# The causal limit of two attentions: from TensorE masks and a VectorE minimum to a position select on GpSimd

## What is computed

```python
xn = layernorm(x)                      # x: 8 batches x 256 tokens x 256
# branch 1 ("MLA"): 16 heads, 64 rotary + 16 plain dimensions
q, k = concat(q_c, rope(q_r)), concat(k_c, rope(k_r))
attn = softmax(q @ k.T * 80**-0.5 + causal mask)
s = (attn @ v) @ w_out.T
# branch 2: rmsnorm, 16 heads of 16 dimensions ("MHA"), then top 2 of 8 experts
attn = softmax(where(causal, q2 @ k2.T * 16**-0.5, -inf))
x2 = xn + (attn @ v2) @ Wo.T
g = silu(x2 + moe(rmsnorm(x2)))
out = x + s * g
```

## Time and profile before

| | us |
|---|---|
| median of 3 runs | 969.01 (966.42 to 970.13) |
| the profiled execution | 961.99 |
| its span, first to last instruction | 960.2 |
| busy in the span: PE, DVE, ACT, POOL | 836.7, 655.9, 502.4, 285.3 |
| one loop iteration (a batch) | 77.3 |

### The profile page before, as it was taken

The page is one execution under the profiler, slowest core; times in us unless marked ns, Lnnn a source line. Parts: engine busy times, 40 slices in busy tenths (PEclk is TensorE's granted clock), DMA queues, the critical chain, the costliest instruction groups (busy, mean ns, idle before and its releaser), DMA issues.

```text
span 960.2 us, 20067 instructions
## 1 busy us (share of the span) xinstructions
PE 836.7 (87%) x6688; PEld 747.9 (78%) x6688; DVE 655.9 (68%) x2335; ACT 502.4 (52%) x1091; POOL 285.3 (30%) x282
## 2 busy tenths in 40 slices
PE   5879999999999998999999999977179999999980
PEld 3868988887887797797898788865169999998980
DVE  4877667667767857866866766763237777777754
ACT  2435365365356356446536535634047777676751
POOL 5520310330221131041032023001314565645641
PEclk9988999999999999999999999988579999999995
DMA  9000000000000000000000000030146677779836
GB/s 277 1 1 1 13 1 25 14 1 13 12 11 2 23 11 2 22 12 1 23 12 1 13 16 7 13 141 15 36 151 184 183 238 202 224 232 334 248 49 186
DMA packets 40159, 70.88 MB, mean 74 GB/s; under 512 B 10946, under 2 KB 35138, under 8 KB 37122
## 3 DMA queue, kind: packets, MB, share of 16 engines
q1 hardware_dynamic: 29074, 57.39, 17.7%
q0 software_dynamic: 9856, 12.13, 6.5%
q10 hardware_dynamic: 1152, 0.49, 0.3%
HBM read 55.25 MB, written 14.81 MB: 73 GB/s over the span
## 4 chain that ended last, share of the span: by engine, by line
PE 51%; DVE 14%; DMA 14%; issue 14%; POOL 3%; ACT 2%; SPq 1%; DVEq 0%; POOLq 0%; ACTq 0%
PE ps L575 40%; DMA expert_rows<-yo,slot_of 11%; PE ps L668 6%; PE ps L705 3%; DVE ps L1400 2%; DVE ps L1403 2%; POOL expert_rows L552 1%; DVE negm L1403 1%; PE ps L601 1%; DMA ln<-in_w_ln 1%; DVE negm L1400 1%; POOL xg L541 1%; PE ps L610 1%; DMA xg<-x_normalised,slot_of 1%; PE ps L805 1%
## 5 line engine op out<-in xcount | busy, mean ns | idle before, releaser
L1094 ACT ACTIVATE ex<-ps 128x384 f32<-128x384 f32 x256 | 125.2, 494 | 130.4 <-PE ps L575 128.9
L575 PE MATMUL ps<-qt,kt 128*128 128x256 f32 (+1 forms) x768 | 163.8, 324 | 4.5 <-issue 3.2
L505 POOL TENSOR_TENSOR tok<-tok,swp 128x256 f32<-128x256 f32 x128 | 97.2, 760 | 219.3 <-DVE swp L1355 218.3
L1400 DVE CUSTOM_DVE_ANT_0 ps<-ps,mask 128x128 f32<-128x128 f32 x256 | 76.2, 298 | 70.4 <-PE ps L575 42.6
L1403 DVE CUSTOM_DVE_ANT_0 ps<-ps,mask 128x256 f32<-128x256 f32 x256 | 118.5, 463 | 0.7
L575 PEld LDWEIGHTS ps<-qt,kt 128*128 128x128 f32 x768 | 109.3, 193 | 11.9 <-issue 7.0
L1234 DVE TENSOR_TENSOR wel<-raw,weh 128x768 fp32r<-128x768 f32 x92 | 88.1, 958 | 34.4 <-ACT weh L962 34.4
L552 POOL DMA_INDIRECT expert_rows<-yo,slot_of x46 | 77.9, 1693 | 104.7 <-DMA expert_rows<-yo,slot_of 54.8
L575 PE MATMUL ps<-wh,xth 128*128 128x320 f32 (+2 forms) x352 | 95.5, 353 | 5.9 <-DVE wl L1234 3.3
L1351 DVE TENSOR_TENSOR tok<-ps,cos_t 128x320 f32<-128x320 f32 x128 | 62.7, 490 | 52.3 <-PE ps L575 46.4
L962 ACT ACTIVATE qt<-ps 128x512 f32<-128x512 f32 (+1 forms) x96 | 57.0, 594 | 61.3 <-PE ps L668 54.6
(11 more groups left out here) (164 smaller groups left out, 1965.8 us busy)
## 6 DMA issues: line engine op xcount, KB each, us to landing
raw<-in_w_experts SPq DMA_DIRECT2D x23, 1536.0 KB, 7.2
mla_branch<-s_b SPq DMA_DIRECT2D x8, 256.0 KB, 2.1
expert_rows<-xn SPq DMA_DIRECT2D x8, 256.0 KB, 2.2
x_normalised<-otk SPq DMA_DIRECT2D x8, 256.0 KB, 2.1
xr<-in_x SPq DMA_DIRECT2D x1, 2048.0 KB, 14.8
s_tok<-mla_branch SPq DMA_DIRECT2D x1, 2048.0 KB, 14.2
w_cols_raw<-in_w_cols SPq DMA_DIRECT2D x1, 1792.0 KB, 15.6
x<-expert_rows SPq DMA_DIRECT2D x3, 512.0 KB, 5.1
```

Source lines behind the costliest of these rows:

```text
L505: nc.gpsimd.tensor_tensor(t, t, swp[:, n % 2, :, :], ALU.add).then_inc(tokd, 1)
L575: return nc.tensor.matmul(o, a, m, start=start, stop=stop, skip_group_check=True, **k)
L1094: nc.scalar.activation(ex[:, h % (2 * G), :], ps[4 + h % 2][:, P:4 * P], ACT.Exp, scale=scale).then_inc(ex_, 1)
L1400: nc.vector.tensor_tensor_reduce(out=o[:, 0:P], in0=o[:, 0:P], in1=mask2[:, 1, :], scale=-1.0, scalar=-2.0 * BIG, op0=ALU.add, op1=ALU.min ...
```

## The change

All 256 diagonal columns of each head's exponentials are limited on POOL, in T1 and in T2, by `affine_select`: it keeps an element where query minus key is not negative and writes 0 elsewhere. T2's `values` therefore wait for a new semaphore `exm2`. DVE's minimum, T2's two mask matmuls a head, two constant loads and two casts go. POOL's order becomes, for each batch: 16 selects of T1 with `power2` after head 6, the 16 rotary sums, 16 selects of T2 with one slot scatter after each of the heads 9, 10, 11 and 12.

```diff
+            def causal(b, ex_, exm, after):
+                for h in range(H):
+                    wait(pool, ex_, 16 * b + h + 1)
+                    pool.nop(nofuse=True)
+                    a = ex[:, h % (2 * G), 0:2 * P].rearrange("p (a q) -> p a q", a=2)
+                    nc.gpsimd.affine_select(a, a, [[0, 2], [1, P]], ALU.is_ge, zero, 0, -1).then_inc(exm, 1)
+                    after.get(h, lambda: None)()
+            def slots_between(r):
+                return {9 + 2 * t + k: lambda t=t, k=k: scatter_slot(r, t, k) for t in range(2) for k in range(2)}
+            zero = nc.gpsimd.to_reg(0.0)
+            causal(0, ex1, exm1, {})
             rope_sums(1)
+            causal(0, ex2, exm2, {})
             pool.wait_ge(s_slot, 16)
             with pool.Fori(1, last) as b:
-                power2(b - 1)
+                causal(b, ex1, exm1, {6: lambda: power2(b - 1)})
                 rope_sums(b + 1)
-                scatter_slots(b - 1)
-            power2(last - 1)
-            scatter_slots(last - 1)
+                causal(b, ex2, exm2, slots_between(b - 1))
+            causal(last, ex1, exm1, {6: lambda: power2(last - 1)})
+            causal(last, ex2, exm2, slots_between(last - 1))
             power2(last)
-            scatter_slots(last)
+            for t in range(2):
+                for k in range(2):
+                    scatter_slot(last, t, k)
...
             def scores2(h, o):
-                mm(o[:, 0:2 * P], kt2[:, h // 2, P:S], qt2[:, h, :], True, False)
-                mm(o[:, 2 * P:4 * P], kt2[:, h // 2, 0:P], qt2[:, h, :], False, False)
-                mm(o[:, P:2 * P], idb[:, :], maskb[:, :], False, True)
-                return mm(o[:, 2 * P:3 * P], idb[:, :], maskb[:, :], False, True)
+                mm(o[:, 0:2 * P], kt2[:, h // 2, P:S], qt2[:, h, :], True, True)
+                return mm(o[:, 2 * P:4 * P], kt2[:, h // 2, 0:P], qt2[:, h, :], True, True)
...
-                heads(b, scores2, st2, ex2, ex2, pv2, ov2, v2, before_h0, lambda: wait(pe, sd, b + 1), max_head,
+                heads(b, scores2, st2, ex2, exm2, pv2, ov2, v2, before_h0, lambda: wait(pe, sd, b + 1), max_head,
...
-            for dst, src in ((idf[:, :], ident), (mask_f[:, 0, :], mask), (mask_f[:, 1, :], mask_t),
-                             (seen[:, 0, :], seen_t), (cos_t[:, :, :], cosines), (sin_t[:, :, :], sines),
+            for dst, src in ((idf[:, :], ident), (mask_f[:, :], mask),
+                             (cos_t[:, :, :], cosines), (sin_t[:, :, :], sines),
...
-            def causal(b, h):
-                wait(dve, ex1, 16 * b + h + 1)
-                a = ex[:, h % (2 * G), 0:2 * P].rearrange("p (a q) -> p a q", a=2)
-                nc.vector.tensor_tensor(a, a, seen[:, 0:1, :].broadcast_to([P, 2, P]), ALU.min).then_inc(exm1, 1)
             def stage_m2(b, after):
                 wait(dve, mtr2, b)
                 for h in range(H):
-                    causal(b, h)
                     maxima(b, h, (h % 2) * (H // 2) + h // 2, negm2, m2d, mx2)
```

More of the change, by code:

```diff
@@ L56 @@
 BIG = -1e30
-BOUND = 1e30
 IT = FF // P
@@ L92, in build @@
 def build(nc, x, w_cols, w_dq, w_uqr, w_dkv, w_ukv, w_out, w_o, w_ln1, w_ln2, w_r, w_experts,
-          cosines, sines, ident, mask, mask_t, seen_t, upper, route_c, slots, out):
+          cosines, sines, ident, mask, upper, route_c, slots, out):
     ctx = ExitStack()
@@ L161, in build @@
         prep = ExitStack()
-        mask_f = sb("mask_f", [P, 2, P], F32, prep)
+        mask_f = sb("mask_f", [P, P], F32, prep)
         up_f = sb("up_f", [P, P], F32, prep)
@@ L171, in build @@
         kt = sb("kt", [P, H, S], F32, early)
-        seen = sb("seen", [P, 1, P], F32, late)
-        idb = sb("idb", [P, P], BF16, late)
-        maskb = sb("maskb", [P, P], BF16, late)
         mask2 = sb("mask2", [P, 2, P], BF16, late)
@@ L263, in build @@
         exm1 = sem("mla_exp_masked")
+        exm2 = sem("mha_exp_masked")
         pv1 = sem("mla_pv")
@@ L513, in power2, with scatter_slot @@
                 nc.gpsimd.tensor_tensor(rstd2[:, :], msq2[:, :], mhalf[:, 0:2], ALU.pow).then_inc(rm2, 1)
-            def scatter_slots(r):
-                pool.wait_ge(posd, r + 1)
-                pool.nop(nofuse=True)
-                for t in range(2):
-                    for k in range(2):
-                        nc.gpsimd.indirect_dma_start(slot[:, :], bass.IndirectOffsetOnAxis(posu[:, t, k:k + 1], 0),
-                                                     meta[:, t, k, :], None).then_inc(msc, 16)
+            def scatter_slot(r, t, k):
+                if t == 0 and k == 0:
+                    pool.wait_ge(posd, r + 1)
+                    pool.nop(nofuse=True)
+                nc.gpsimd.indirect_dma_start(slot[:, :], bass.IndirectOffsetOnAxis(posu[:, t, k:k + 1], 0),
+                                             meta[:, t, k, :], None).then_inc(msc, 16)
+            def causal(b, ex_, exm, after):
+                for h in range(H):
+                    wait(pool, ex_, 16 * b + h + 1)
+                    pool.nop(nofuse=True)
+                    a = ex[:, h % (2 * G), 0:2 * P].rearrange("p (a q) -> p a q", a=2)
[5 more added lines that the diff above has]
+            causal(0, ex1, exm1, {})
             rope_sums(1)
+            causal(0, ex2, exm2, {})
             pool.wait_ge(s_slot, 16)
             with pool.Fori(1, last) as b:
-                power2(b - 1)
+                causal(b, ex1, exm1, {6: lambda: power2(b - 1)})
                 rope_sums(b + 1)
-                scatter_slots(b - 1)
-            power2(last - 1)
-            scatter_slots(last - 1)
+                causal(b, ex2, exm2, slots_between(b - 1))
+            causal(last, ex1, exm1, {6: lambda: power2(last - 1)})
+            causal(last, ex2, exm2, slots_between(last - 1))
             power2(last)
-            scatter_slots(last)
+            for t in range(2):
+                for k in range(2):
+                    scatter_slot(last, t, k)
             def gather(blk):
@@ L864, in _ @@
                 if m == 1:
-                    pe.wait_ge(s_k, 16 * 8)
+                    pe.wait_ge(s_k, 16 * 6)
                     transpose_x(0)
@@ L884, in _ @@
             pe.wait_ge(s_c, 16 * 4)
-            pe.wait_ge(cast, 3)
+            pe.wait_ge(cast, 1)
             for h in range(H):
@@ L997, in _ @@
                                      scale=ln1[:, m:m + 1]).then_inc(wfh, 1)
-            act.wait_ge(s_k, 16 * 8)
-            copy(idb[:, :], idf[:, :]).then_inc(cast, 1)
-            copy(mask2[:, 1, :], mask_f[:, 0, :])
-            copy(maskb[:, :], mask_f[:, 1, :]).then_inc(cast, 1)
+            act.wait_ge(s_k, 16 * 6)
+            copy(mask2[:, 1, :], mask_f[:, :])
             copy(upb[:, :], up_f[:, :]).then_inc(cast, 1)
@@ L1152, in _ @@
             act.wait_ge(wdonep, 1)
-            act.wait_ge(cast, 3)
+            act.wait_ge(cast, 1)
             act.wait_ge(wdone, N_DIRECT)
@@ L1559, in gates @@
                 nc.vector.tensor_tensor(g[:, :, 1], gexp[:, :], gsum[:, :], ALU.mult).then_inc(posd, 1)
-            dve.wait_ge(s_k, 16 * 8)
+            dve.wait_ge(s_k, 16 * 6)
             dve.wait_ge(clear, 2)
@@ L1732, in laid_out @@
     slots[:, 1] = T + np.arange(SLOTS)
-    consts = dict(cosines=cosines, sines=sines, ident=np.eye(P), mask=mask, mask_t=mask.T, seen_t=np.where(i[:, None] > i[None, :], 0.0, BOUND),
+    consts = dict(cosines=cosines, sines=sines, ident=np.eye(P), mask=mask,
                   upper=i[:, None] < i[None, :], route_c=route_c)
```

## The result

| | before | after |
|---|---|---|
| median of 12 runs on the same chips | 965.53 us (962.62 to 970.13) | 971.17 us (968.98 to 972.31) |
| ratio to before, 95% interval | | 1.0057 [1.0039, 1.0074] |
| span of the profiled execution | 960.2 us | 969.3 us |

The changed kernel is slower by 0.57%, 5.6 us. The time forecast, 971, is the time measured, but that is half luck: the forecast stood on a median of 969.01 for before, which came out at 965.53 over more runs, and to that it added a change of 1.4 us where 5.6 came. The forecast was "within 0.5%"; the measurement is just beyond that, and its interval reaches across it. More important, the terms of the sum are not those that the trace shows.

A forecast was written before the change was run, and what follows sets the result against it. PE was taken to set most of the time. Six iterations +0.3, batch 0 -1.0, last batch +2.4, start -0.3 made +1.4 on 961.99: 963.4; with 7.0 for the runs' median, about 971 us, range 957 to 987 (8 in 10).

The forecast's parts named there:

- T1: First stage: removing DVE's minimum closes PE idle that DVE causes, -1.2 us an iteration, bounds 0.7 and 1.3.
- near the upper bound, since gaps too small to be listed go too: Reason for taking 1.2 us in T1: unlisted small PE gaps would close as well as the visible 0.58 us wait.
- Masks: T2: removing mask matmuls from PE; only six pairs up to head 9 count, bringing it forward 0.6 us.
- T2's tail on POOL: End of T2: selects 10 to 15 queue behind four scatters, delaying the last values and the transposes by 1.55 us.
- held DVE instructions: T2: DVE's small steps and one rounding lie beside POOL's selects; 0.3 us added for one held instruction.
- d: Time of one select on POOL: 0.55 us taken, low end 0.33, high end about 1.3.
- 0.9 us of it later the transposes start: End of T2: values(3) moves from 530.04 to 532.0, so transposes of the maxima start at 532.9 instead of 531.34.
- 4.6 us that were forecast: Last batch's T2: select 15 ends at 666.9 against 662.3 for the second half of the values, +4.6 us.
- the estimate worked out from it for a select: From the skill page's line rate and 1.2 GHz: 0.21 us plus fixed cost, giving a sum near 957 us.
- 0.1 us of d is 4.9 us of the kernel: Whole kernel: 49 selects lie in POOL's tails, so the select's price was said to decide the case.
- first rival: Cheap select: POOL's T2 tail shrinks, kernel faster at 956 to 964 us for d under about 0.45; chance 0.30.
- The lock: Rival: POOL holds DVE throughout T2 through a shared path, T2 +2.5 us, kernel about 980 us; chance 0.09.

The follow-up runs named there:

- all_masks_and_dve_list: The changed kernel with T2's mask matmuls kept for all 16 heads and 16 filler memsets in place of DVE's minimum; 1.0063 of before.
- t1_alone_list_kept: Kernel before with only T1's selects on POOL replacing DVE's minimum, and 16 filler memsets where the minimum stood; 0.9948 of before.
- dve_start_moved: The changed kernel with 16 filler memsets on DVE once, ahead of the loop, putting the loop's start back at 485; 1.0023 of before.
- start_moved_scatters_5: The changed kernel with 16 filler memsets ahead of DVE's loop and all four scatters after T2's select of head 5; 1.0001 of before.
- start_moved_scatters_15: The changed kernel with 16 filler memsets ahead of DVE's loop and all four scatters after T2's last select, next to the turn; 1.0071 of before.
- dve_list_kept: The changed kernel with 16 filler memsets in place of DVE's minimum, in batch 0 and in the loop body; 1.0014 of before.
- masks_kept_0_to_5: The changed kernel with T2's two mask matmuls a head kept for heads 0 to 5; 1.0052 of before.

## Why the prediction came out as it did

**T1: right in kind, 0.35 us too much.** -0.85 us an iteration in every kernel, against -1.2 and bounds of 0.7 and 1.3. The visible wait for `negm` of 0.58 us went; the choice "near the upper bound, since gaps too small to be listed go too" was the error: 0.49 us of PE idle stay. PE waited for no select in T1, as forecast.

**Masks: a little low.** 0.6 us an iteration was forecast; with the selects in both, they are worth 0.89 at the full clock, 5.3 in six, and the medians show 3.9 (971.73 to 967.85).

**T2's tail on POOL: mis-sized by a wide margin.** Forecast +1.55 and +0.3 for held DVE instructions; measured +0.26 together in T2 at the full clock (all_masks_and_dve_list against t1_alone_list_kept), some 0.18 of it by the scatters' place. Four things were off: d 0.425 instead of 0.55; no 0.1 us before a select that is already released (three in a row take 1.19 us); no 0.30 us behind a scatter when a select follows; and the step "0.9 us of it later the transposes start", which made all of POOL's delay the stage's. DVE's last maxima end within 0.1 us of the `values`, so most of that delay lies beside DVE's. In the last batch the tail shows, though shorter than the 4.6 us that were forecast. PE in order of time, after, where before `values(3)` follows at once, as the second half of the row at 661.59:

```profile
667.33 1.08 PE L588 MATMUL ps<-ex,v 128*32 128x256 f32 x8 [3.01 <-POOL ex L525]
```

The half as a whole was not cheap: 11.4 us by the medians of these two kernels, but most of it at the turns, in low stretches and in the last batch, and not in T2 where the sum had it.

The page "GPSIMD Engine Reference" of the Trainium skill, section "Engine selection", calls one-input operations on GpSimd roughly line rate; the estimate worked out from it for a select was 0.21 us and a fixed cost, about 0.31 in all. No trace here agrees: 0.414 to 0.425. The 0.1 us of fixed cost in it stands in no row of this case either.

**The select's price did not decide.** The text made it so ("0.1 us of d is 4.9 us of the kernel") and gave "faster" for d under about 0.45. d was 0.425 and the kernel was slower. The first rival's condition came true and its result did not.

**The lock: rival refuted.** Roundings at a median of 419 ns, T2 short when the clock is full.

**The turn of the loop: no term at all, +5.5 us.** The change removes 16 DVE instructions from batch 0 and the body; no number of the forecast rested on where a list's loop starts or ends. That DVE's restart is later is shown: the copy's input lies there for 2.8 us. That the place of the loop in the list makes it so is shown by dve_start_moved, which changes that and no other thing: some 0.9 us a turn. What the place does, the instruction queue's packets show: two at the turn instead of one. That scatters near the turn add to it is shown by start_moved_scatters_5 against dve_start_moved: the packet takes 0.31 to 0.49 us instead of 1.28 to 1.59, and the restart comes 2.73 to 2.96 us after the branch instead of 3.23 to 3.56. The pause of start_moved_scatters_15 is another thing, a late word from PE. The Trainium skill, page "Runtime: NRT & Kernel Launch", section "Instruction fetch mechanics", says that engines load their lists in blocks of 256 instructions through a DMA queue of their own, that crossing a block costs little, and that a taken branch out of the window forces a load before execution goes on. This trace agrees with the queue and with a load behind the jump (535.38 in after). It differs in the size, 8 KB and some 125 places of the list apart for DVE, and in the cost where a block is crossed right at the jump.

**The low clock: no term either, +9 us in this profile.** In T2 it stood in 6 of 6 iterations of after and 0 of 6 of before, and each costs 1.5 us (21.53 against 20.02 in dve_start_moved, 22.18 against 20.65 above). With -0.6 for T2 at the full clock, 6 x (1.5 - 0.6) = 5.4 is the +5.0 of the table and a little more. The text had seen "the last batch's T2 runs partly at the low TensorE clock" and priced the masks there by it, but never asked whether it could come to the other batches. What decides it is open. In kernels with mask matmuls at T2's head it stood in 10 of 36 iterations, in those without in 35 of 48. PE work was taken from a place just before and beside a wait of PE, so the masks may have kept the clock up. Much speaks against making them the cause. The counts come from one execution of each kernel. all_masks_and_dve_list has 4 of 6 with every mask in place, as many as dve_list_kept without them, and is 3.9 us slower. In masks_kept_0_to_5 the low stretches moved to the turns. Two iterations of one kernel with equal rows differ. And before has its low stretches too: each execution's mean granted clock is on record, and in 35 executions of before on one chip the shortest (960.50 us) has 0.952 and the longest (969.77) 0.944; the mean is over the whole kernel and does not say where the low stretches lie. The profile of before, 961.99 us at 0.952, is a short one, so its 0 of 6 is at the low end. After is lower in all 12 of its executions, 0.931 to 0.938. The medians of the other kernels with masks at T2's head are 0.938 to 0.952 and of those without 0.932 to 0.940, and masks_kept_0_to_5 is the 0.938; its profile, with 0.943, is the shortest of its six executions. So the masks are a possible part of it, not a shown one.

**So the sum.** The two unseen terms, +5.5 and +9, were offset by an overpriced tail: +1.85 was taken for what costs 0.26 an iteration, 9.5 us in six. 971 was right in number, and would have been some 10 us lower had the tail in T2 been priced as it is.

## What to carry to other kernels

Taking work off an engine also changes where its loop begins and ends in its list, and an engine that must restart quickly at the turn can lose more by it than the work was worth: compare the pause at the turn before and after, count the packets of the instruction queue between the branch and the restart, and try a few cheap filler instructions ahead of the loop. Keep POOL's indirect DMAs away from the turn. When the trace names the one that ended a wait, look up in the kernel which count the instruction waits for: here PE stood beside a pause that DVE's restart made. Judge the halves of a change apart, on one chip: here T1's half gained 0.5% (5.3 us) once the turn was repaired, and T2's half took 7.6 us (dve_list_kept against t1_alone_list_kept), although the masks that it took from PE were worth 3.9.

## What was unexpected of the hardware

- A loop of DVE that ends at place 833 of its list, with a packet of the instruction queue due near 835, has two instruction packets at each turn instead of one, and restarts 3.2 to 4.5 us after the branch. The kernels whose loop ends elsewhere restart after 2.7 to 3.1 us without scatters nearby and 2.9 to 4.3 us with them.
- The first packet of the instruction queue that starts up to 4.3 us after a scatter of POOL took 0.9 to 2.2 us nearly every time; the packets far from scatters took 0.31 to 0.9 us, 0.44 in the median.
- While POOL issues indirect DMAs (0.96 to 1.03 us each), the word that PE has finished can come late: 0.8 to 3.3 us after the matmuls' recorded end, with waits of 0.55 to 2.27 us on PE behind it. In before, with the same four scatters, none was over 0.5 us late; what decides it is open.
- The low clock stood for 3.41 or 3.42 us nearly every time, cost 1.5 us each in T2, and came in one iteration and not in the next with the same rows ahead of it.
